# A chunked state-space layer: the two steps of a slot taken from neighbouring head groups instead of from one

## The reference, cut to what matters

```python
proj = x @ W_in.T + b_in                       # gate | h,B,C | dt
conv = sum(xp[:, i:i+S, :] * conv_w[:, i] for i in range(4))
hBC  = silu(conv); h, Bm, Cm = split(hBC)
dt   = softplus(dt + dt_bias); Adt = -exp(A_log) * dt
# per chunk:
#   Y_diag = (C B^T * exp(segsum(Adt)) masked) @ (h * dt)
#   state  = exp(sum Adt) * state + (B * decay)^T @ (h * dt)
#   Y_off  = C * exp(cumsum Adt) @ state
y = (Y_diag + Y_off + D * h) * silu(gate)      # then RMS-normed over 2,048, @ W_out.T
```

## Time and profile before

| | |
|---|---|
| median of 3 runs | 2259.94 us (2259.93 to 2260.1) |
| the profiled execution's own time | 2262.73 us |
| its span, first to last instruction | 2261.0 us |
| PE / DVE / ACT / POOL busy in the span | 94 / 70 / 56 / 63 % |
| mean granted TensorE clock | 0.986 of 2.4 GHz |

### The profile page before, as it was taken

How to read it: one execution, slowest core, us unless ns; L and a number is a source line. 1 busy time by engine, 2 the same in 40 slices (tenths; PEclk the granted TensorE clock), 3 DMA queues, 4 the chain that set the end, 5 groups by cost and what they waited for, 6 DMA issues and landing times. The chain is left out here.

```text
span 2261.0 us, 43811 instructions
## 1 busy us (share of the span) xinstructions
PE 2124.2 (94%) x13681; PEld 1685.8 (75%) x13681; DVE 1575.2 (70%) x3408; ACT 1266.4 (56%) x2754; POOL 1414.6 (63%) x1248
## 2 busy tenths in 40 slices
PE   4878999999999999999999998999989989999997
PEld 2446777777777777777777776877744779999997
DVE  5778888888888888888888884676766853333332
ACT  2456777777777777777777772222235653333332
POOL 1325777777777777777777775777764624444443
PEclk9999999999999999999999999999999999999999
DMA  9854445545554455454545544886473065232221
GB/s 321 333 135 119 135 144 147 152 137 146 145 156 135 144 148 151 139 146 143 150 140 145 141 133 140 254 268 217 151 261 118 1 222 137 48 50 47 46 46 24
DMA packets 193458, 328.83 MB, mean 145 GB/s; under 512 B 49043, under 2 KB 135188, under 8 KB 192980
## 3 DMA queue, kind: packets, MB, share of 16 engines
q1 hardware_dynamic: 135972, 227.40, 34.1%
q0 software_dynamic: 26640, 53.38, 9.1%
q10 hardware_dynamic: 30624, 45.25, 6.5%
HBM read 240.19 MB, written 86.53 MB: 145 GB/s over the span
## 5 line engine op out<-in xcount | busy, mean ns | idle before, releaser
L1014 DVE SCALAR_TENSOR_TENSOR m_cv<-m_hp,conv,m_cv 128x256 f32<-128x256 f32 x864 | 416.7, 482 | 112.2 <-ACT m_cv L913 91.0
L840 POOL TENSOR_TENSOR m_er<-m_er,m_cT 128x1024 f32<-128x1024 f32 x128 | 302.3, 2362 | 43.7 <-DVE m_ar L1021 43.7
L951 ACT ACTIVATE m_ar<-m_ar,m_ta 128x128 f32<-128x128 f32 x1024 | 318.9, 391 | 0.8
L1102 PE MATMUL m_hp<-xnT,wpj 128*128 128x259 f32 x1152 | 304.7, 387 | 7.8 <-PEq L145 4.5
L1110 PE MATMUL m_gp<-xnT,wpj 128*128 128x256 f32 x1024 | 268.2, 384 | 11.2 <-ACT m_gT L931 11.2
L1538 PE MATMUL e_u<-e_xgT,xnT 128*128 128x128 f32 x2272 | 266.9, 276 | 1.0 <-ACT xnT L1476 1.0
L1102 PEld LDWEIGHTS m_hp<-xnT,wpj 128*128 128x128 f32 x1152 | 214.1, 192 | 68.7 <-issue 28.3
L1538 PEld LDWEIGHTS e_u<-e_xgT,xnT 128*128 128x128 f32 x2272 | 260.9, 193 | 1.3 <-ACT xnT L1476 1.2
L847 POOL TENSOR_TENSOR m_hdd<-m_hdt,m_tb 128x512 f32<-128x512 f32 x128 | 131.0, 1043 | 193.6 <-DVE m_hdt L1029 193.6
L931 ACT ACTIVATE m_gT<-m_gp,bias 128x256 f32<-128x256 f32 x256 | 121.4, 474 | 230.6 <-PE m_gp L1110 178.5
L1161 PE MATMUL m_out<-wo,m_gT 128*128 128x256 f32 x1024 | 242.9, 380 | 0.0
(11 more groups left out here) (338 smaller groups left out, 4260.8 us busy)
## 6 DMA issues: line engine op xcount, KB each, us to landing
m_ar<-acum_rows_dram SPq DMA_DIRECT2D x512, 128.0 KB
m_er<-eacum_rows_dram SPq DMA_DIRECT2D x128, 512.0 KB, 4.3
rows_by_slot<-blank_rows ACTq DMA_DIRECT2D x1, 18576.0 KB, 81.0
e_xg<-rows_by_slot ACTq DMA_DIRECT2D x131, 129.0 KB
m_xrow<-xn_rows SPq DMA_DIRECT2D x32, 512.0 KB, 5.1
arena<-y_rows SPq DMA_DIRECT2D x16, 1024.0 KB, 7.2
arena<-in_w SPq DMA_DIRECT2D x5, 1024.0 KB
wpj<-in_w_proj SPq DMA_DIRECT2D x1, 4352.0 KB, 23.6
```

The lines of the kernel that those rows point to most:

```text
L840: g.tensor_tensor(er[:, t], er[:, t], middle(cT[:, t * P:(t + 1) * P], HQ), ALU.mult).then_inc(scaled.sem, 1)
L951: ins = a(row, row, ACT.Exp, bias=ta[:, t, q * HQ + h:q * HQ + h + 1])
L1014: v_.scalar_tensor_tensor(o, hp[n % 2][:, j:j + BLK], conv[:, c, j:j + 1], o, ALU.mult, ALU.add).then_inc(tapped.sem, 1)
L1102: ins = mm(hp[n % 2][:, 0:PW], w_proj[:, kd, col:col + P], xpad[:, kd, ds(i * BLK, PW)], start=kd == 0, stop=kd == KD - 1)
```

## The change

Steps are numbered through the head groups; a slot now does the step t = 1 of head group n-2 (`older(n - 1)`, called a) and the step t = 0 of head group n-1 (`newer(n - 1)`, called b). The two belong to different head groups, so neither needs the state of the other. For each engine the order in a slot is new:
- PE: `from_state`, `inside` of a, then of b, directly behind each other, `update` of a, the sixth chunk, `project_out` of a, `update` of b. The `project_out` of the step b of the slot before moves forward, half of it into c = 2 and half into c = 3. `add_up` comes one slot later (U1 in place of U0).
- DVE: the mixes stand behind the third `keep`; both `finish` come first, then `grow` of a, the last taps, `grow` of b.
- POOL: `scale` of b, sums of squares, `weigh` a and b, `age` a and b, and at the end `scale` for the next slot's a. The wait for the mixes is gone.
- ACT: exponentials of the next slot's pair; the last `first_tap` of a slot comes behind all sixteen exponentials, where two of the second eight preceded it. The copy of `out_ps` waits for the `project_out` of a in U0.
- SP: the decay rows and row matrices go in the order of the new pairs.
- The small per-block tables `ta`, `tb`, `gm`, `btok` get a third place, since tile 1 of a block is used one slot longer. One slot more drains (DEPTH 3).
No arithmetic is added or removed.

```diff
-DEPTH = 2
+DEPTH = 3
...
+def older(m):
+    return divmod(m - 1, NQ) + (1,) if 0 < m <= NB * NQ else None
+def newer(m):
+    return divmod(m, NQ) + (0,) if 0 <= m < NB * NQ else None
+def pair(m):
+    return [s for s in (older(m), newer(m)) if s]
+def kept(i, t):
+    return 1 + i % 2 if t else 0
...
@@ SP
-                    for t in range(TB):
-                        s = q * TB + t
-                        off.wait(sp, i, s - 1)
...
+                    for i, q, t in pair(n):
+                        decay_rows(i, q, t)
+                        row_matrix(i * STEPS + q * TB + t + TB)
@@ POOL
+                    a, b, last = older(n - 1), newer(n - 1), newer(n - 2)
+                    if b:
+                        scale(*b)
+                    if last:
+                        add_squares(*last)
+                    if a:
+                        weigh(*a)
+                    if b:
+                        weigh(*b)
+                    if a:
+                        age(*a)
+                    if b:
+                        age(*b)
+                    if last and last[1] == NQ - 1:
+                        fold_squares(last[0], 0)
                     if u:
-                        i, q = u
-                        mixed.wait(pool, i, q * TB + TB)
-                        scale(i, q, 0)
-                        weigh(i, q, 0)
-                        weigh(i, q, 1)
-                        age(i, q, 0)
-                        scale(i, q, 1)
...
+                        scale(*u, 1)
+                    if a:
+                        add_squares(*a)
+                        if last_of(a):
+                            fold_squares(a[0], 1)
@@ ACT
-                    for t, lead in enumerate((1, 2)):
-                        if w:
-                            exps(*w, t, range(0, lead))
-                            first_tap(w[0], late[t])
-                            exps(*w, t, range(lead, HQ))
+                    for step, chunk in ((older(n), 0), (newer(n), 1)):
+                        lead = HQ if chunk else 1
+                        if step:
+                            exps(*step, range(0, lead))
+                        if late[chunk] is not None:
+                            first_tap(w[0], late[chunk])
+                        if step and lead < HQ:
+                            exps(*step, range(lead, HQ))
...
+                    if last_of(older(n - 2)):
+                        i = older(n - 2)[0]
                         ss_done.wait(act, i, 1)
@@ DVE
-                    if u:
-                        mix(*u, 0)
-                        mix(*u, 1)
                     for c in range(CQ):
                         if u:
                             keep(*u, c)
                         if soon[c] is not None:
                             taps(w[0], soon[c])
+                        if c == 2 and a:
+                            mix(*a)
+                        if c == 2 and b:
+                            mix(*b)
                     if w:
                         taps(w[0], late[0])
-                    if u:
-                        grow(*u, 0)
-                        finish(*u, 0)
+                    if a:
+                        finish(*a)
+                    if b:
+                        finish(*b)
+                    if a:
+                        grow(*a)
                     if w:
                         taps(w[0], late[1])
-                    if u:
-                        finish(*u, 1)
-                        grow(*u, 1)
+                    if b:
+                        grow(*b)
@@ PE
+                        if c >= 2 and last:
+                            project_out(*last, range(c * 2 - 4, c * 2 - 2))
...
-                    if u:
-                        from_state(*u, 0)
-                        inside(*u, 0)
-                        update(*u, 0)
+                    for step in pair(n - 1):
+                        from_state(*step)
+                        inside(*step)
+                    if a:
+                        update(*a)
                     if w:
                         project(w[0], late[1])
-                    if v:
-                        project_out(*v, 1)
-                    if u:
-                        from_state(*u, 1)
-                        inside(*u, 1)
-                        update(*u, 1)
-                    if v and v[1] == NQ - 1:
-                        add_up(v[0])
-                    if u:
-                        project_out(*u, 0)
+                    if a:
+                        project_out(*a)
+                    if b:
+                        update(*b)
+                    if last_of(older(n - 2)):
+                        add_up(older(n - 2)[0])
```

More of the change, by code:

```diff
@@ L707, in at, with both, last_of @@
             return (i, q) if 0 <= i < NB else None
-        body(at(0), at(1), at(2))
+        body(n, at(0), at(1))
+def older(m):
[6 more added lines that the diff above has]
+    return 1 + i % 2 if t else 0
+def both(i):
+    return slice(0, 2 + i % 2, 1 + i % 2)
+def last_of(step):
+    return step is not None and step[1] == NQ - 1 and step[2] == TB - 1
 def ssd_phase(nc, sem, k, xpad, w_proj, w_out, bias, conv, d_col, dt, tabs, acum_dram, eacum_dram, ss, mo_dram,
@@ L950, in exps, with body @@
                         row = ar[:, s % 4, h, :]
-                        ins = a(row, row, ACT.Exp, bias=ta[:, t, q * HQ + h:q * HQ + h + 1])
+                        ins = a(row, row, ACT.Exp, bias=ta[:, kept(i, t), q * HQ + h:q * HQ + h + 1])
                     if heads[-1] == HQ - 1:
                         ins.then_inc(exped.sem, 1)
-                def body(w, u, v):
-                    soon, late = fresh(w[1]) if w else ([None] * 4, [])
+                def body(n, w, u):
+                    soon, late = fresh(w[1]) if w else ([None] * 4, [None] * 2)
+                    last = newer(n - 2)
                     if u:
@@ L981, in body @@
                         act.dma_start(tokens(mo_dram, i * TB, TB), mo[:]).then_inc(s_mo, 16)
-                    if u:
-                        square(*u, 0)
-                    if v and v[1] == NQ - 1:
-                        i = v[0]
+                    if step:
+                        square(*step)
+                    if last_of(older(n - 2)):
+                        i = older(n - 2)[0]
                         ss_done.wait(act, i, 1)
@@ L1053, in finish, with body @@
                     v_.tensor_tensor(gg, gg, y1[:].rearrange("p (c l) -> p c l", l=P), ALU.mult).then_inc(gated.sem, 1)
-                def body(w, u, v):
-                    soon, late = fresh(w[1]) if w else ([None] * 4, [])
+                def body(n, w, u):
+                    soon, late = fresh(w[1]) if w else ([None] * 4, [None] * 2)
+                    a, b = older(n - 1), newer(n - 1)
                     if w and w[1] == 0:
-                        exped.wait(dve, w[0], 0)
-                        v_.tensor_copy(ta[:], tabs[:, ds(w[0] * TB, TB), 0, :]).then_inc(ta_done.sem, 1)
+                        i = w[0]
+                        exped.wait(dve, i, -1)
+                        v_.tensor_copy(ta[:, both(i)], tabs[:, ds(i * TB, TB), 0, :]).then_inc(ta_done.sem, 1)
                     if u and u[1] == 0:
@@ L1152, in inside, with project_out @@
                     ins.then_inc(diag.sem, 1)
-                def project_out(i, q, t):
+                def project_out(i, q, t, chunks=range(CQ)):
                     s = q * TB + t
@@ L1158, in project_out @@
                         mok.wait(pe, i, 0)
-                    for c in range(CQ):
+                    for c in chunks:
                         cc = q * CQ + c
```

85 lines of the change are left out of this document (42 added, 43 removed).

## The result

The changed kernel takes 2337.39 us in the median of four runs (2332.1 to 2342.74), the kernel before took 2260.02 on the same chip (2259.93 to 2262.82). The ratio is 1.0332 with a 95% interval of 1.0302 to 1.0363: slower by 3.3%. The forecast was slower by 1.5%, and the time lies 5 us above the upper end of the range. The profiled execution took 2342.74 us, 80.0 more than that of before. Of these, 71.2 lie between the first and the sixteenth transposition of B and C (L1169; 167.4 to 1302.8 us before, 164.0 to 1370.6 after), and 8.8 in what lies around them. A block, from one such transposition to the next, took 75.03 us and takes 80.54 (mean of the last fourteen, from 77.75 to 82.36). The first interval is apart: 85.04 us before and 79.13 after, so 5.9 us shorter. The profiled execution is the slowest of its four.

The account below looks back on a forecast made before the run. PE was taken to bound the kernel. Slots summed to a block of 76.9 us for 75.03; 16 blocks added 30 us and the drain 4, giving a median of 2294 us, 1.5% slower, with an 8 in 10 range of 2225 to 2332.

Parts of the forecast that it names:

- The keeps and the pairing: On PE: waits behind late keeps, 3.9 us a block, all go; pairing half-wide products saves 0.2 us a slot.
- the borders: PE entering half-wide products (0.09 us) and leaving them (0.1 to 0.2); one of each per slot, saving 0.2 a slot.
- The seam: PE between `inside` of a and `from_state` of b; if it hides no more than before, 12 us higher in sum.
- the third rival: Set up with the experiments, not the prediction: PE's new order costs something by itself; no size or chance given.
- the forecast's main term: PE at `update` of b waits for `grow` of a: 1.65 us in U2 and U3, 1.0 in U0 and U1.
- a collision: DVE's product of b comes 0.3 us behind the start of POOL's `scale` and is held off; PE stands 1.65 us.
- The hold-off's own measure: On DVE: a product held off by POOL's `scale` ends 0.55 us behind the end of that `scale`.
- ACT's late copies and `gm`: PE's transpositions wait: 0.5 us for `gm` in U0, 0.7 behind ACT's late sums and SiLU in U2.
- E: The end of `from_state` of a on PE, from which the prediction counts times within a slot.
- rival C: Mixes on DVE, taking turns with POOL's products, delay everything behind them: block 79.6 us, median 2337; chance 0.14.
- the sum's line: Adds the slots U3 20.3, U0 19.05, U1 18.3 and U2 19.25 us to a block of 76.9, 1.9 more.
- The count around the blocks: Whole kernel: 16 blocks add 30 us, and the longer drain of DEPTH 3 adds 4 (0 to 8).

Follow-up runs that it names:

- the control: Kernel before, order untouched, with the sum of `finish` written into the PSUM bank: 2249.47 us for 2249.81, ratio 1.0001.
- the run of the mixes alone: Changed kernel with POOL waiting for the mixes before all but `scale` of b: 2347.43 us, ratio 1.0375 to the kernel before.
- the copies: Changed kernel with ACT's sums copied before squaring, `add_up` ahead of the sixth chunk, `out_ps` copied next slot behind the first SiLU: 2319.2 us, ratio 1.0231.
- POOL's order: Changed kernel with POOL's indirect DMAs behind `scale` of b and `weigh` of a, sums of squares behind the mixes: 2326.81 us, ratio 1.028.

## Why the prediction was right and wrong, step by step

**The keeps and the pairing: right.** No transposition waits for a `keep` behind the mixes. Sets of half-wide products now follow each other (`inside` to `from_state` starts 102 ns apart, like two pairs of records within a set). The waits that went are some 3.3 us a block instead of 3.9, and the borders save 1.0, forecast 0.8. The seam hides its weight load; what the prediction weighed as a cost of 12 us more by a strict reading of the Trainium skill (TensorE: Matmul & The Clock Gate, The mechanism) did not come. PE's work without a wait is 70.5 to 70.8 us a block in all nine traces of the table, where the forecast had 70.4. That is 0.3 of the 3.6 us that the forecast lacks in a block. The kernel before had 71.7, so the third rival, that PE's new order costs something by itself, is out.

**`update` of b: right in mechanism, a little small.** This was the forecast's main term: 5.3 us a block, measured 6.2. Three runs take it away in different ways (another order on DVE, another memory, POOL waiting) and each time most of the loss goes; the control shows that the held product by itself is harmless. The missing 0.9 lies in U0 and U1, for which the forecast took 1.0 each, halfway between a collision and none. Between 300 and 1300 us the stalls, with what the lower clock adds inside them, have means of 1.6 in U0, 1.5 in U1, 1.5 in U2 and 1.9 in U3. They are not regular: in U0 eight are 2.3 and four 0.2, as between 823 and 826 us above, where the rows landed late. The hold-off's own measure, 0.55 behind the end of `scale`, was exact. The forecast gave U3 0.9 with nothing held off; the run with `scale` behind the product has 0.9 there too, with a's product still held off by `age`.

**ACT's late copies and `gm`: 1.3 for 1.2, in part by luck.** `gm` costs 0.2 and not 0.5, and the SiLU 1.1 and not 0.7. The forecast said that the copy of `out_ps` would cost 1.2 in U1 where `update` of b has not waited, and nothing where it has. That is what the runs show: with the sum in PSUM or grow first the wait in U1 is 1.5 us, in the changed kernel 0.4 in the mean.

**The output of a behind the sixth chunk: missed.** I had a's product end at E + 3.65 and PE at the output at E + 4.7, with no wait. Where the mixes are held off, everything on DVE moves back and PE waits for `gated`: 0.7 us a block, gone in both runs that free most of the mixes. This is rival C's mechanism at about a quarter of the 2.7 a block that stood between C and the forecast (79.6 and 76.9).

**The clock: missed, and the largest error.** The prediction reads the clock of the kernel before, at its upper level throughout, and prices every distance of the new order by it, without asking what the new stalls would do. 1.6 us a block are lost at 1.2 GHz, some 22 us of the 80 in the profiled execution.

**The step that failed is the sum's line "A block is 76.9 us for 75.03".** It is 3.6 too small: 1.6 for a clock that it held at 2.4 GHz, 0.9 at `update` of b, 0.7 at the output, for which it had nothing, 0.3 in PE's work and 0.1 at the transpositions.

**The count around the blocks was wrong too, the other way.** The forecast counts 16 blocks of the same gain or loss and 4 us for the ends, 34 us in all. The trace has 14 intervals 5.5 us longer (77), a first one 5.9 shorter, and 8.8 around them, together 80. By the forecast's own way 16 x 5.5 + 4 would be 92.

**The number of rival C came true, its cause did not.** C's 2337 us rested on mixes held off by POOL's products in every slot. Of the 128 mixes 84 began beside no product of POOL, and freeing the others gave back 0.5% in one run (the intervals touch) and nothing in another. That its time agrees to the microsecond is luck: its block is 79.6 us for 80.5, and its count of blocks makes up for it. Had only the time been looked at, it would have passed for the explanation.

What stays open: why the run of the mixes alone has the higher ratio, 1.0375 for 1.0332. The intervals touch, its block is only 0.2 us longer, with some 0.4 more lost at 1.2 GHz, and its first interval 1.7 us; the rest was not followed.

## What to carry to other kernels

When an order is changed so that an instruction that frees a buffer of the bottleneck engine stands behind one more instruction, ask what can hold that one off, and put the freeing one first if it costs nothing. A VectorE product with two SBUF inputs beside GpSimd's products is such a one, and keeping one of its inputs in PSUM cured it here. Price a stall of some two us on TensorE at more than two: in the changed kernel many were followed by a stretch in which the matmuls took twice as long. And several small stalls on one path cover each other, so what a remedy gains alone is not what it gains beside others: the copies gained 1.0% alone and 1.6% behind another remedy, the grow and POOL's order 0.6% each and 0.4% together at the end.

## What the runs showed of the hardware that was not expected

**A wait of some 2 us can lose the upper clock, but need not.** Between 300 and 1300 us of the changed kernel the clock falls twelve times, and PE's last long wait ahead of the fall is between 1.89 and 2.36 us in eleven of them and 1.45 in one. Of its thirteen waits of 2 us or more eight are followed by a fall, and the longest, 2.8, is not. The run with `scale` in the next slot has 38 waits of 1.5 to 1.9 us in that stretch and no fall; the run with `scale` behind the product has no wait above 1.0 us and none either. What decides in between was not followed.

**Who gets ahead when both wait is not a matter of who asked first.** The mix at 833.56 waits for the `scale` that runs until 835.30, and then POOL's next product, `weigh` at 835.24, goes ahead of it, at its full speed; the mix takes 3.83 us for 1.21. This happened in all five cases of the changed kernel where a mix waited for a `scale` and `weigh` was ready, and in all fifteen of the kernel with grow first. DVE's product with 512 columns was not passed in the changed kernel: in 25 cases it waited for a `scale` with a sum of squares behind it, and was served between the two. It isn't a fixed rule by instruction: with POOL's order only, one such product (at 451.67) was passed by an `age` behind an `age`, and mixes were served between two of POOL's products, two of them in the run with the sum in PSUM and the copies (at 281.75 and 864.97), each behind a sum of squares. The prediction had expected `weigh` between the two mixes, not ahead of a mix that already waited. The Trainium skill (SBUF — State Buffer, Who interferes with whom) has issue order decide; these mixes had asked first. What makes the difference was not tried.
